# Expert routing moved into the shared experts' rounds, shared weights split in the attention stage

## What is computed

```python
x = x + attention(layernorm(x))                      # x1
xf = layernorm(x)                                    # 8192 rows of 256
xn = layernorm(xf) * ln_scale + ln_bias
probs = softmax(xn @ gate_w.T)                       # 8 experts
tk_probs, tk_idx = top_k(probs, 2)
tk_probs = tk_probs / (sum(tk_probs) + EPS)
out = swiglu(xf, sWg, sWu, sWd)                      # shared expert, all rows
for e in range(8):
    out = out + w[:, e:e+1] * swiglu(xf, Wg[e], Wu[e], Wd[e])
x = x + out
```

## Time and profile before

| what | value |
| --- | --- |
| median of 3 runs | 2199.15 us (2195.25 to 2200.13) |
| the profiled execution's own time | 2204.27 us |
| its span, first to last instruction | 2202.6 us |
| PE busy | 1975.4 us, 90% of the span |
| mean granted TensorE clock | 0.972 of full speed |
| attention stage | 0 to 1191 us |
| routing | 1191 to 1231 us |
| shared expert and scatter | 1232 to 1534 us |
| experts | 1534 to 2203 us |

### The profile page before, as it was taken

How to read it: one execution, slowest core, us unless ns; L and a number is a source line. 1 busy time by engine, 2 the same in 40 slices (tenths; PEclk the granted TensorE clock), 3 DMA queues, 4 the chain that set the end, 5 groups by cost and what they waited for, 6 DMA issues and landing times. The chain is left out here.

```text
span 2202.6 us, 48214 instructions
## 1 busy us (share of the span) xinstructions
PE 1975.4 (90%) x14698; PEld 1300.5 (59%) x14767; DVE 1252.1 (57%) x3885; ACT 1081.8 (49%) x2354; POOL 790.8 (36%) x1150
## 2 busy tenths in 40 slices
PE   2789999999999999999984499997999999999997
PEld 1344445454444554454542388886777777777776
DVE  5556677666667666667653554553444545454544
ACT  1155555555555555555542355542555555555553
POOL 2023323333333333233331155540344444444443
PEclk9989999999999999999986699999999999999999
DMA  7124443444443444443311365652783333333332
GB/s 206 43 82 117 133 129 114 125 118 117 132 128 114 123 118 116 134 128 110 121 53 51 132 206 196 210 179 71 214 212 58 54 52 59 54 58 56 56 53 36
DMA packets 156640, 246.08 MB, mean 112 GB/s; under 512 B 29408, under 2 KB 90592, under 8 KB 156480
## 3 DMA queue, kind: packets, MB, share of 16 engines
q1 hardware_dynamic: 120960, 189.24, 27.9%
q0 software_dynamic: 32064, 53.44, 11.6%
q10 hardware_dynamic: 3456, 1.34, 0.2%
HBM read 111.89 MB, written 90.50 MB: 92 GB/s over the span
## 5 line engine op out<-in xcount | busy, mean ns | idle before, releaser
L631 DVE CUSTOM_DVE_ANT_0 ps_rows<-ps_rows,maskrow 128x512 f32<-128x512 f32 (+3 forms) x1024 | 484.4, 514 | 308.7 <-PE ps_rows L488 307.9
L576 ACT ACTIVATE probs<-ps_cols 128x512 f32<-128x512 f32 (+3 forms) x1024 | 392.1, 435 | 394.7 <-PE ps_cols L499 388.0
L488 PE MATMUL ps_rows<-ks,qs 32*128 32x512 f32 (+3 forms) x2048 | 429.7, 494 | 85.4 <-DVE mx L631 48.0
L495 PE MATMUL ps_cols<-qs,ks 32*128 32x512 f32 (+3 forms) x2048 | 422.0, 488 | 2.5 <-ACT probs L576 2.4
L1597 POOL DMA_INDIRECT out_dram<-y_e,to x135 | 215.6, 1597 | 349.1 <-DMA out_dram<-y_e,to 210.7
L750 POOL TENSOR_TENSOR pace<-eps 1x1 f32<-1x1 f32 x256 | 58.2, 227 | 786.3 <-ACT probs L576 786.3
L488 PEld LDWEIGHTS ps_rows<-ks,qs 32*128 32x128 f32 x2048 | 162.2, 188 | 295.9 <-DVE mx L631 246.9
L499 PE MATMUL ps_cols<-mT,ones_r 32*128 32x512 f32 (+3 forms) x1024 | 287.4, 554 | 0.0
L1726 DVE TENSOR_TENSOR h_lo<-ps_h,h_hi 128x512 fp32r<-128x512 f32 x135 | 93.4, 692 | 231.0 <-ACT h_hi L1701 231.0
L1695 ACT ACTIVATE sg_e<-ps_ge 128x512 f32<-128x512 f32 x135 | 80.7, 598 | 261.3 <-PE ps_ge L1619 259.4
L512 PE MATMUL ps_o<-probs,vt 128*32 128x512 f32 (+3 forms) x2048 | 193.7, 450 | 0.8 <-POOL probs L752 0.8
(11 more groups left out here) (207 smaller groups left out, 3732.3 us busy)
## 6 DMA issues: line engine op xcount, KB each, us to landing
xs_d<-zrows SPq DMA_DIRECT2D x45, 408.0 KB, 2.9
xr<-xs_d POOLq DMA_DIRECT2D x135, 136.0 KB, 3.0
whi_d<-w_sh SPq DMA_DIRECT2D x16, 768.0 KB, 3.8
w_hi<-whi_d SPq DMA_DIRECT2D x24, 512.0 KB
xn<-in_L_attn_x_dram SPq DMA_DIRECT2D x16, 512.0 KB, 5.4
ks<-k_lin SPq DMA_DIRECT2D x64, 128.0 KB, 3.1
ks<-k_tan SPq DMA_DIRECT2D x64, 128.0 KB, 3.8
qs<-q_lin SPq DMA_DIRECT2D x64, 128.0 KB, 2.4
```

The source lines that it names most:

```text
L488: mm = nc.tensor.matmul(ps_rows[bank_of(row_no(g, it, h))][:, 0:(it + 1) * P], qs[at:at + STRIP, d.par, g, it * P:(it + 1) * P], ks[at:at ...
L495: nc.tensor.matmul(ps_cols[bank_of(col_no(n, s, e))][:, jt * P:S], ks[at:at + STRIP, b.par, gc, jt * P:(jt + 1) * P], qs[at:at + STRIP, b. ...
L576: nc.scalar.activation(probs[:, n % 2, 2 * (1 - s) + e, jt * P:S], ps_cols[bank_of(col_no(n, s, e))][:, jt * P:S], ACT.Exp).then_inc(exp_d ...
L631: nc.vector.tensor_tensor_reduce(out=bank, in0=bank, in1=maskrow[:, (TT - 1 - it) * P:S], scale=1.0, scalar=LOWEST, op0=ALU.add, op1=ALU.m ...
```

## The change

`route_stage` and `scatter_stage` become one block, `front_stage`.

- The shared weights are loaded in the attention stage's prologue, behind the first loads of x, into three buffers that are not used there yet (`osb`, `o_val`, `o_inv`), and POOL splits them in six operations before its first work on a batch. ACT's first write to `osb` waits for the six. The split weights stay on chip.
- In the new block PE starts with the gate sums and the logits' transposes as before, but into banks of the shared expert, then goes on with the transposes of batch 0 and the rounds. The two counting matmuls stand in round 2 between column blocks 0 and 1, in the two banks of the transposes (`ps_t`); PE waits for `rank_taken` before it turns the next batch.
- DVE's routing chain is laid between the units of rounds 0 to 3 by hand (`beside()` runs the next unit).
- The exponential stands on ACT behind round 0.
- Row tiles start in round 4, with `A_ROUND` = (2, 1, 2, 1). Four batches of rows are loaded ahead in place of three. The row buffers' padding is cleared by POOL.

```diff
+        for m, src in enumerate(shared_weights):
+            sp.dma_start(shared_st[m].rearrange("p (k n) -> p k n", k=IT if m == 2 else KT), src.rearrange("(k p) n -> p k n", p=P))\
+                .then_inc(shared_in, 16)
...
+        pool.wait_ge(shared_in, 3 * 16)
+        for m in range(3):
+            nc.gpsimd.tensor_copy(shared[m][:, 0], shared_st[m]).then_inc(shared_split, 1)
+        pool.wait_ge(shared_split, 3)
+        for m in range(3):
+            nc.gpsimd.tensor_tensor(shared[m][:, 1], shared_st[m], shared[m][:, 0].bitcast(F32), ALU.subtract).then_inc(shared_split, 1)
...
-    FIRST, RING, AHEAD = NB, 8, 3
-    A_ROUND = (1, 1, 1, 2)
+    FIRST, RING, AHEAD, RANK_AT, ROWS_AT = NB, 8, 4, 2, 4
+    A_ROUND = (2, 1, 2, 1)
...
-        pe.wait_ge(se.w_lo, 3)
-        rounds(lambda s: se.tensor_round(pe, s))
+        for s in range(FIRST + 1):
+            if s == RANK_AT:
+                se.tensor_round(pe, Batch(0, s), ranks, ranks_taken)
+            else:
+                se.tensor_round(pe, Batch(0, s))
...
-        se.split_weights_hi(act)
         se.copies(act, Batch(0, 0))
-        rounds(lambda s: se.scalar_round(act, s, norm_rows))
+        for s in range(FIRST + 1):
+            se.scalar_round(act, Batch(0, s), norm_rows)
+            if s == 0:
+                act.wait_ge(exp_in, 1)
+                nc.scalar.activation(prob[:], a[:], ACT.Exp).then_inc(exp_out, 1)
...
+        choose(prob, m1, oh[0])
+        then(nc.vector.scalar_tensor_tensor(out=b[:], in0=oh[0][:], scalar=-2.0, in1=prob[:], op0=ALU.mult, op1=ALU.add))
+        choose(b, m2, oh[1])
+        tt(rank[:], oh[0][:], oh[1][:], ALU.add).then_inc(chosen, 1)
+        beside()
...
+        beside()
+        dve.wait_ge(ranked, 1)
+        nc.vector.tensor_copy(b[:], ps_n)
+        then(nc.vector.tensor_copy(rank[:], ps_r))
+        nc.vector.nop(nofuse=True).then_inc(rank_taken, 1)
```

More of the change, by code:

```diff
@@ L1204, in sem @@
         return nc.alloc_semaphore(name)
+    row = [sb(f"row{q}", [P, 2, XW]) for q in range(RING)]
+    xw = sb("xw", [P, AHEAD, TT, D])
     rr = sb("rr", [P, NT])
@@ L1245, in route_stage, with tiles_of, _, load_rows @@
     pos_ready = sem("pos_ready")
+    se = SharedExpert(nc, ctx, sbt, "_1", 0, FIRST, shared, x1_d, out, ident, mv2, rstd2)
     block = ctx.enter_context(nc.Block())
+    ps_s = se.ps_y[0][:, 0, 0:2 * NE].rearrange("p (c e) -> p c e", c=2)
+    ps_l = [bank[:].rearrange("p (b t) -> p b t", t=P) for bank in (*se.ps_g, *se.ps_u)]
+    ps_r, ps_n = (bank[:].rearrange("p (t e) -> p t e", e=NE) for bank in se.ps_t)
+    def tiles_of(s, i):
+        n = sum(A_ROUND)
+        first = (s.off - ROWS_AT) * n + sum(A_ROUND[:i])
+        many = A_ROUND[i] if s.off < FIRST - 1 else 2
+        return range(max(first, 0), min(first + many, NT)) if s.off >= ROWS_AT else range(0)
+    @block.sync
+    def _(sp):
+        def load_rows(bt):
+            if bt >= AHEAD:
+                sp.wait_ge(normed, (bt - AHEAD + 1) * TT * 2)
+            sp.dma_start(xw[:, bt % AHEAD], x1_d[bt]).then_inc(xw_loaded[bt % AHEAD], 16)
+        se.load_in(sp, Batch(0, 0))
+        se.load_in(sp, Batch(0, 1))
+        se.load(sp, Batch(0, 0))
+        se.load(sp, Batch(0, 1))
+        se.load_in(sp, Batch(0, 2))
+        for bt in range(AHEAD):
+            load_rows(bt)
+        loaded = AHEAD
+        for s in range(FIRST + 1):
+            if s >= 1:
+                se.load_in(sp, Batch(0, s + 2))
+            while loaded < NB and (loaded - AHEAD + 1) * TT <= (s - ROWS_AT) * sum(A_ROUND):
+                load_rows(loaded)
+                loaded += 1
+            se.store(sp, Batch(0, s - 1))
+            if s >= 1:
+                se.load(sp, Batch(0, s + 1))
+        for bt in range(loaded, NB):
+            load_rows(bt)
+        for r in range(2):
+            sp.wait_ge(se.y_stored[r], (FIRST + 1 - r) // 2 * 32)
     @block.tensor
@@ L1273, in _ @@
         nc.gpsimd.memset(lower[:], 1.0).then_inc(filled, 1)
+        for q in range(RING):
+            nc.gpsimd.memset(row[q][:, :, D:XW], 0.0).then_inc(cleared, 1)
         pool.wait_ge(filled, 1)
@@ L1287, in _ @@
         n = [0]
+        units = [0]
         def then(ins):
@@ L1293, in then, with beside @@
             dve.wait_ge(chain, n[0])
+        def beside():
+            s, i = divmod(units[0], IT)
+            units[0] += 1
+            se.vector_unit(dve, Batch(0, s), i)
+            if i == IT - 1 and se.has(Batch(0, s)):
+                se.lower(dve, Batch(0, s), IT - 1)
         def over_e(ap):
@@ L1345, in _ @@
         choose(b, m2, oh[1])
+        tt(rank[:], oh[0][:], oh[1][:], ALU.add).then_inc(chosen, 1)
+        beside()
+        assert units[0] == RANK_AT * IT
         then(tt(cc[:], m1[:], m2[:], ALU.add))
@@ L1492, in expert_stage @@
+        while units[0] < (FIRST + 1) * IT:
+            beside()
 def expert_stage(nc, ctx, sbt, whi_d, wlo_d, xs_d, out, ident, slot_e):
```

256 lines of the change are left out of this document (97 added, 159 removed).

## The result

The changed kernel took **2181.61 us** (median of 4 runs, 2181.01 to 2184.37) against 2197.94 us for the kernel before beside it: a ratio of 0.9928, 95% interval 0.9915 to 0.9941. It is faster, as forecast, but by 16 us in place of 41, and 12.6 us above the range. The profiled execution spans 2182.7 us, that of before 2202.6. Further down, one execution of e1_five (4624 us) and one of h1_five (2805 us) fell into a slow state of the chip; their medians of four include it, their ratios don't.

The account below looks back on a forecast made before the run. PE, busy 90% of the span, plus its gaps was taken as the bound, chiefly the routing gap. Savings 42.6 - 0.7 (block ends) - 0.5 (start) = 41.4 us, so 2199.15 - 41.4 = 2157.8 us; range 2150 to 2169.

Parts of the forecast that it names:

- The start of PE: New block: first gate products at 1199.7 in place of 1246.45, with weights already on chip, 46.7 us earlier.
- Counting and its waits: Round 2: counting matmuls put 2.2 us into PE's path, plus waits of 1.0 us for `chosen` and 2.5 for `rank_taken`.
- The rival that DVE slips: Rounds 0 to 3: DVE becomes the bound; 2162 us if its path is a tenth longer, 2168 if a quarter; chance 0.17.
- The clock: First gate products: 2.3 us lost at half clock come back, or 1.0 of them is hidden; savings 43.3 or 42.0, middle 42.6.
- the better case: First gate products: PE's upper clock level holds, so 2.3 us come back and savings are 43.3 us.
- The table of ScalarE: Exponential in new block: one more table change, 1.29 us by the trace; the skill's 2.66 us would make the sum 40.2.
- Ends and start: Block's end with semaphore clearing comes again, 0.7 us; three more loads at kernel start, 0.5 us within bounds 0 and 3.
- Row tiles: Rounds from 4: six tiles in place of five; POOL's twelve transfers need 16.0 of 17.6 us, so cost 0.
- the threshold of 1.47: Rounds 4 to 14: time per POOL transfer, with its pause, at which twelve transfers fill a 17.6 us round.
- The prediction's own sign of being wrong: PE waits for `h` or `sg` in rounds 0 to 3, rounds from 4 exceed 17.6, or attention ends over 3 us after 1191.
- POOL becomes the bound: Rounds 4 to 14: slower POOL transfers hold ACT, then PE; at 2.0 us each 68 us lost, 2226 us; chance 0.03.
- The sum: Whole kernel: 42.6 - 0.7 - 0.5 = 41.4 us saved, from median 2199.15 to 2157.8 us; forecast itself has chance 0.62.

Follow-up runs that it names:

- e1_five: Changed kernel with row tiles one, one, one, two a round (five) from round 3 on, first group: 2155.56 us, 0.9787 of the kernel before.
- h1_five: Changed kernel at five row tiles a round from round 3 on, on a fourth-group chip without the waits: 2155.02 us.
- g1_after_third: Changed kernel, word for word, on the third group's chip without the waits: 2154.13 us, 0.9802 of the kernel before.
- f1_after_again: Changed kernel, word for word, repeated on the second group's chip, which shows the waits: 2180.10 us, 0.9911 of the kernel before.
- i1_after: Changed kernel, word for word, a fourth time, on the fifth group's chip, which shows the waits: 2176.71 us, 0.9890 of the kernel before.
- f4_order: Changed kernel with one, two, one, two row tiles a round in place of two, one, two, one: 2171.04 us, 0.9870 of the kernel before.
- f2_before_again: Kernel before, word for word, repeated for its trace on the second group's chip, which shows the waits: 2198.45 us.
- the third group: One chip without the waits; changed kernel unchanged 2154.13 us, at five tiles a round 2155.52, without later row loads or without POOL's row transfers 2156.06 and 2153.05.
- i3_noload: Changed kernel without the twelve later loads of rows, on the fifth group's chip with the waits: 2171.93 us, 0.9873 of the kernel before.

## Why the prediction missed, point by point

- **The start of PE: right, a little short.** From the block's first operation to the second down product it took 92.98 us before, 46.90 after and 46.73 in g1_after_third: 46.1 to 46.3 us saved. The prediction had 46.7 - 2.2 - 3.5 + 1.6 = 42.6. Gate products came at 7.8 and 7.6 us into the block where 8.4 was worked out.
- **Counting and its waits: right in place, over in size.** The counting lies between the first two down products, and these are 20.98 us apart, 3.44 more than 17.54, where 5.7 was forecast. The two counting products cost 2.0, `chosen` was met without a wait (1.0 forecast), `rank_taken` cost 1.46 (2.5 forecast). DVE had `chosen` 39.4 us into the block where its walk gave 41.6, and PE stood there at 39.9. The rival that DVE slips did not come.
- **The clock: the better case.** Six gate products took 1.65 us from the first on, not 2.90 as in the earlier trace rows: the 2.3 us came back. The reading of the earlier trace rows was a little off: a mean of 0.90 with 0.50 in the us behind it means that the clock fell at 1199.8 and not 1199.9, still behind 1199.7.
- **The table of ScalarE.** The exponential's load ran 1.28 us, and the operation followed 1.29 after its start, as in the earlier trace rows:

```profile
1211.11 1.28 ACT L1333 ACT_TABLE_LOAD   x1
...
1212.40 0.64 ACT L1333 ACTIVATE prob<-ra 128x512 f32<-128x512 f32 x1
```

  The Trainium skill, "ScalarE: Activation LUTs", section "What ACT_TABLE_LOAD costs", adds a drain of about 1380 ns to this; neither trace shows one, and the measurement decides. ACT's operation before this load ended at 1211.09, so there is no room for it ahead of the load either.
- **Ends and start.** From the last down product to the load of `w_hi` took 9.41 us before, 10.01 after and 11.51 in g1_after_third (0.7 more was forecast). 1.5 us of the latter are the clock. In windows of one us of g1_after_third, PE alone, the last down product falls to the lower level, 1.2 GHz, after PE had stood 2.17 us ahead of it, and takes 7.50 us. In the kernel before and in after PE stood as long there, the clock stayed up, and the product took 6.02.

```profile
1473.00:1474.00 1.00, 0.94 (x5) 0.71 0.00 0
1474.00:1475.00 1.00, 1.00 (x6) 0.50 0.00 0
```

  The start cannot be told from 0: the block begins at 1191.3, 1181.4 and 1187.7 us in three traces of the old start, and at 1181.4 to 1191.8 in those of the new.
- **Row tiles, "Cost 0": the step that failed.** It asked whether POOL has time for twelve transfers in a round, found 16.0 of 17.6 us, and was right in that: POOL never was the bound, its mean pace in a run of twelve was 1.30 to 1.41 us, and the threshold of 1.47 was not reached. It did not ask what the others wait for while POOL's run goes on. The answer stood in the trace of before. Of its waits from 1250 to 1490 us (total, times, longest) this was passed over, since no round was longer for it:

```profile
DVE ysb L1178 <- remote: 36.2, 12, 3.7
```

  With eight transfers, the last 5.9 us behind the product, DVE's second addition came at 8.4 us and was covered. With twelve, the last up to 9.8 behind, it came at up to 12.5 and was not covered. The term put at nothing measured 28.3 us in after, 24.5 in f1_after_again and 17.4 in i1_after, and nothing in g1_after_third. The prediction's own sign of being wrong, rounds from 4 on longer than 17.6, came true. In the rival "POOL becomes the bound" the count was the right suspect with the wrong mechanism and a chance of 0.03. The rule that it cites of the Trainium skill, "SBUF — State Buffer", section "Who interferes with whom", is about POOL's transfers being held up by DVE. The traces bear it out in part: in before all 13 transfers that start while DVE makes `x2n` took 1.59 or 1.60 us where most take 0.96, and the mean of the earlier trace rows holds them; in the longer rounds of after such a transfer took 1.0. But what made the time longer was DVE, ACT and PE standing.
- **The sum.** With the block at 343.15 us before and 325.93 after, the change brought 17.2 us there, and the rest of the 19.9 between the spans are 1.45 of an earlier start of the block and 1.2 of a shorter expert stage (666.9 us; the new kernels' traces have 666.4 to 668.1). In g1_after_third, without the waits, the block takes 299.09 us: 44.1 saved, where 41.9 was forecast for it, and the median is 42.2 below the kernel before beside it (2196.30), where 41.4 was forecast. That it comes so near is in part luck: the start gave 3.6 us more than forecast, and the end of the block took 1.4 more. The range had no case for a chip with the waits.

**What stays open.** Which part of the chip holds the engines back while POOL issues transfers, and why the waits are there in two groups and not in the other three. Each group had its own chip, so chip and time can't be told apart, and what ran on the chips' other cores isn't on record. Within a group all traces agree. f4_order shows that the end of the run isn't all of it: with runs of twelve that end 10.2 to 10.5 us behind the product the second half comes at 8.7 to 9.2 in most rounds. Leaving out the transfers was not seen on a chip with the waits, so that they make the waits isn't shown by taking them away. It rests on the rounds without any in after and f2_before_again (5.95 to 6.04 us, in one trace with rounds of 8.4) and on the wait's moving with the end of the run. Fetching of instructions is unlikely: by the record of DMA queues no packet of it lies between 1305 and 1324 us in after, which has two such waits.

**The version to keep** is five tiles a round from round 3 on. Ratios 0.9787, 0.9801, 0.9793 and 0.9809 to the kernel before in four groups, of which one was on a chip with the waits; the changed kernel there had 0.9890. Where there are no waits the two are the same (2155.52 and 2154.13 us in the third group).

## What to carry to other kernels

A wait that costs nothing because it is covered is still a term of the sum as soon as the change raises what it grows with; list the covered waits beside a resource that is to be used more, those with no named releaser above all, and set the longest against the slack. Where an engine issues DMAs of its own beside a tight loop, leave slack for them: five tiles a round were free on all four chips where they ran, six on some only. When an experiment undoes an effect, run the unchanged kernel beside it on the same chip, or the chip may have undone it.

## What the runs showed of the hardware that was not expected

- The same program differs from one group to another, each on its own chip. On three chips no trace of this program (eleven, five kinds of kernel) has a wait for "remote" in the rounds; on two all seven have, as have the first traces of before and after. It is 2154.13 us against 2176.71 and 2180.10 for the same code, while the kernel before is at 2196.3 to 2199.8 in all five groups.
- Where the waits show, DVE's and ACT's starts and PE's own issue are held beside back-to-back transfers of POOL. ACT stood up to 9.6 us before it was let go by "remote", where it stands 5.7 at the same place in g1_after_third; DVE stood up to 8.0. In the rounds shown of after and i3_noload the two were let go within 0.1 us of each other. POOL's pace of 1.26 us does not suffer.
- 6.3 MB of loads on the same DMA engines (busy share of a round 0.63 with them, 0.49 without) changed the stretch by 0.02 us.
